# A three-layer graph network with a feed-forward block on one core: f32 tables and one f32 product per gathered tile, in place of three bf16 parts and two products

## Chip, core and metric

One core of one Trainium2 chip runs the whole program in one launch. The metric is the device time in microseconds. The kernel before has a median of 7058.9 us over three runs (7055.39 to 7071.32).

## The reference

12500 nodes with 256 features, 200000 edges sorted by destination. Three graph layers and one feed-forward block, both residual:

```python
def _sage_layer(x, src, dst, inv_deg, W_self, W_neigh, b):
    agg = jax.ops.segment_sum(x[src], dst, num_segments=N_NODES)
    mean = agg * inv_deg[:, None]
    return x @ W_self + mean @ W_neigh + b
h = relu(layer0(layernorm(x)));  h = relu(layer1(h));  h = layer2(h);  x = x + h
# then: x = x + gelu(layernorm(x) @ w1 + b1) @ w2 + b2, scaled, for the rows with the largest x @ wr
```

The destinations are drawn as 12500 u², so low-numbered nodes have far more edges than high-numbered ones.

## The kernel before

The nodes are worked on in 98 windows of 128 (NT). The edges are cut in 1563 tiles of 128, and the tiles in 391 blocks of four (GROUP). For each layer there is a table in DRAM with one row per node. GpSimd gathers, with one indirect DMA per tile (line 672), the 128 source rows of a tile into `gath`, a ring of 16 tiles (RING, four blocks). VectorE makes for each tile a one-hot matrix of 128 edges by 128 nodes of the window (lines 1223 and 1230), and TensorE adds the tile's rows to their nodes as the product of that one-hot with the gathered rows, into the PSUM bank `agg` of the window.

Products on f32 data are not used for this. Each f32 row x is held as three bf16 parts: high = bf16(x), middle = bf16(x - high), low = the rest, so a table row is 3 x 256 bf16, or 1536 bytes. A tile takes two products: line 890 multiplies the one-hot with high and middle (512 columns), line 892 with low (256 columns; 257 in layer 0, where the last column counts the edges of each node). In layer 0 the low product has a bank of its own, `lo`, which ScalarE copies out (line 1716) before the next window may clear it (lines 878 and 879).

Phase 0 loads x, layer-normalises it in batches of four windows into `resid` (ScalarE, line 1678), and makes the three parts: casts on ScalarE (lines 1684 and 1690), subtractions on VectorE (lines 1085 and 1094). Batches are stored to `table[0]` on ScalarE's DMA queue (line 1702), and the gathers begin when all are stored.

In the layers, each window w is worked on in a slot of a loop over windows: the products of window w's blocks, and beside them the finishing of windows w-1 to w-4. Layer 0 divides the sum by the degree in `mean_done` (lines 1243 to 1260). The layer's matrix products are TensorE's lines 731, 743, 756 and 718. A product's left half is the next layer's table row, its right half the part that the node adds to itself. `copy_product`, `copy_rest` and `store_parts` (ScalarE, lines 1588 to 1616: copy L1596, casts L1597 and L1604, a store of the f32 row to `rows_f32` and one of the three parts to the table) and `split_product` (VectorE, lines 1183 to 1197: subtractions L1191 and L1196, bias L1193) make the parts. In layers 1 and 2 `aggregate_done` adds high and middle sums to the rest in two steps (lines 1276 and 1284).

The blocks of a window run from `first` to `shared`, the block that the window border cuts. TensorE's and VectorE's loops (line 898 and below line 1230) take one block a turn, in two or four spans (`sub_spans`, line 416), between which other work of the slot is issued. The shared block stands behind the loops. Its gathered rows are used by both windows, its one-hots are made once for each. The one-hots of block b lie in ring place (b + w) % 4, an address worked out at run time by both engines. A block that is done raises `slots_free`. Before VectorE makes a block's one-hots it waits for `slots_free` to reach the block's number plus a base (2 in layer 0). GpSimd waits for the same semaphore before it gathers into a block's place, through a relay on SyncE's queue, which also loads the gather indices (lines 600 to 605).

Layer 0 makes in windows 2 to 33 a second thing: counts of edges between groups of nodes. VectorE makes one-hots for them (lines 1340 and 1342), TensorE multiplies (line 784), ScalarE copies out (line 1623). With them layers 1 and 2 do the first four windows as dense products (line 827) with the f32 rows read from `rows_f32`, and skip those windows' gathers: layer 0 has 1564 gathers, layers 1 and 2 have 1260 each. Layer 2 has the feed-forward block in its slots: line 959 (256 to 1024), gelu on ScalarE (line 1795), line 969 (1024 to 256). A last stage picks the rows and stores the result.

Of the kernel before, what the change touches and what calls it, by code (L numbers as in the profile page):

```python
# [7 lines left out]
ALU = mybir.AluOpType  # L8
# [6 lines left out]
P = 128  # L15
PARTS = 3
# [8 lines left out]
FIN_BUFS = 19  # L25
# [5 lines left out]
COUNT_AT = 2  # L31
COUNT_LOOPED = 6
# [4 lines left out]
def gnn_ffn_program(nc, x, src, dst, w_self, w_neigh, b_gnn, wr, br, w1, b1, w2, b2, out):  # L37
# [68 lines left out]
    table = [nc.dram_tensor(f"table{l}", (N, PARTS * D), BF16).ap() for l in range(LAYERS)]  # L106
    idx_dram = nc.dram_tensor("idx_dram", (P, PADDED + TURN_TILES), I32).ap()
    rows_f32 = [None] + [nc.dram_tensor(f"rows_f32_{l}", (N, D), F32).ap() for l in range(1, LAYERS)]
# [3 lines left out]
    with ExitStack() as ctx:  # L112
# [11 lines left out]
        gath = sb("gath", [P, RING, PARTS * D + 2], BF16)  # L124
        onehot = sb("onehot", [P, RING, P], BF16)
# [26 lines left out]
        lo_sb = [sb(f"lo_sb{p}", [P, D + 1]) for p in range(2)]  # L152
# [5 lines left out]
        def build_area(cols):  # L158
# [23 lines left out]
        split = [sb(f"split{p}", [P, PARTS, D], BF16) for p in range(2)]  # L182
# [21 lines left out]
               for area, bufs in ((dense[:], 6), (gath[:].rearrange("p r d -> p (r d)").bitcast(F32), 6), (dst_f[:], 1),  # L204
# [4 lines left out]
        FIN_AFTER_SUMS, FIN_AFTER_FFN = 6, 13  # L209
# [13 lines left out]
        agg_lo = lo0[:]  # L223
# [13 lines left out]
        flag = split[1][:].rearrange("p t d -> p (t d)").bitcast(F32)[:, 0:NT]  # L237
        rest4 = [hidT[p][:].rearrange("p k n -> p (k n)").rearrange("p (b d) -> p b d", d=D) for p in range(2)]
# [55 lines left out]
        y32_stored = [sem(f"y32_stored{p}") for p in range(2)]  # L294
# [17 lines left out]
        hi4_ready = sem("hi4_ready")  # L312
        rest4_ready = sem("rest4_ready")
        mid4_ready = sem("mid4_ready")
        lo4_ready = sem("lo4_ready")
        shift4_ready = sem("shift4_ready")
        half_added = sem("half_added")
        lo_added = sem("lo_added")
        lo_copied = sem("lo_copied")
        mid_added = sem("mid_added")  # L320
# [20 lines left out]
        hi_ready = sem("hi_ready")  # L341
        rest_ready = sem("rest_ready")
        self_ready = sem("self_ready")
        mid_ready = sem("mid_ready")
        lo_ready = sem("lo_ready")
# [290 lines left out]
        def _(pool):  # L636
# [17 lines left out]
            for layer in range(LAYERS):  # L654
# [4 lines left out]
                else:  # L659
                    for k in range(4):  # L660
                        pool.wait_ge(slots_stored[k], 16 * (1 + BATCHES // 4 + (k < 2)))
# [1193 lines left out]
```

## Time and profile before

| | |
|---|---|
| median of three runs | 7058.9 us |
| profiled execution | 7076.15 us |
| its span | 7074.4 us, so 1.8 us lie outside |
| mean granted TensorE clock | 0.802 |
| busy: TensorE, VectorE, ScalarE, GpSimd | 4579, 2607, 1085, 3887 us |

The page gives busy times per engine and per line. PE is the matmul part of TensorE, PEld its weight loads, DVE is VectorE, ACT ScalarE, POOL GpSimd, SP SyncE; a name with q behind it is the engine's sequencer. "<-" names what ended an idle time; "issue" means that the engine waited for nothing that the profile shows, "remote" that the release came from outside it. The stages in time: phase 0 to 149 us, layer 0 to 2940, layer 1 to 4870, layer 2 with the feed-forward block to 6970, the last stage to 7074.

### The profile page before, as it was taken

Reading aid. Unit: us, or ns where it says so; the run is one execution under the profiler, and the core shown is the slowest. Engines: PE = TensorE matmul, PEld = TensorE weight load, DVE = VectorE, ACT = ScalarE, POOL = GpSimd, SP = SyncE. Lnnn points to the kernel's source line nnn. Section 1 sums busy time; section 2 is a strip of 40 time slices with the busy share of each in tenths; the row PEclk is TensorE's granted clock in tenths of the full one; section 3 lists DMA queues with packets and bytes.
Section 4 is the critical chain, followed back from the end, with each engine's and each line's share of the span. In section 5 each row is a group of like instructions: output and inputs, shape, how many; then the busy total and the mean of one; then the engine's idle time right before and its main releaser. Section 6 shows DMA issues by size and latency. Waiting matters only on the chain.

```text
span 7074.4 us, 108443 instructions
## 1 busy us (share of the span) xinstructions
PE 4579.0 (65%) x20873; PEld 2778.3 (39%) x20874; DVE 2607.1 (37%) x6727; ACT 1084.7 (15%) x2649; POOL 3887.2 (55%) x4094
## 2 busy tenths in 40 slices
PE   1444555555667777646778656665578998788884
PEld 0112222222333344323456222222256776566664
DVE  6123333444423333311222332333333444455556
ACT  5000001111111112100000000000011223223331
POOL 1654544444466666566666666665666664555551
PEclk9666677777777888767888777777689998989997
DMA  7443444444455555446666555554456664444445
GB/s 232 133 116 109 123 121 124 126 126 126 129 143 146 150 151 151 145 135 185 192 197 208 157 151 147 155 156 137 133 181 187 194 197 116 135 139 136 125 129 181
DMA packets 564997, 1065.13 MB, mean 151 GB/s; under 512 B 154587, under 2 KB 361983, under 8 KB 558527
## 3 DMA queue, kind: packets, MB, share of 16 engines
q0 software_dynamic: 261376, 803.21, 39.9%
q10 hardware_dynamic: 196564, 228.51, 9.5%
q1 hardware_dynamic: 106987, 32.54, 2.0%
q8 instruction: 37, 0.61, 0.0%
q14 instruction: 33, 0.27, 0.0%
HBM read 928.09 MB, written 135.83 MB: 150 GB/s over the span
## 4 chain that ended last, share of the span: by engine, by line
issue 35%; PE 29%; DVEq 10%; DVE 7%; another core or an unknown queue 6%; POOL 5%; ACT 4%; DMA 1%; ACTq 1%; SPq 0%; POOLq 0%
PE agg L890 10%; POOL gath L672 5%; PE y L969 3%; PE agg L892 3%; PE lo L892 2%; PE hid L959 2%; PE y L731 2%; DVEq L1347 2%; PE lo L827 2%; DVEq L1240 1%; DVEq L1340 1%; ACT hidT L1795 1%; DVEq L1223 1%; PE hid L756 1%
## 5 line engine op out<-in xcount | busy, mean ns | idle before, releaser
L672 POOL DMA_INDIRECT gath<-table,idx_ring x4084 | 3885.7, 951 | 3052.3 <-issue 1344.3
L890 PE MATMUL agg<-gath,onehot 128*128 x5216 | 2262.5, 459 | 1392.3 <-issue 1036.4
L890 PEld LDWEIGHTS agg<-gath,onehot 128*128 x5216 | 578.4, 111 | 2287.9 <-issue 1999.8
L892 PE MATMUL agg<-gath,onehot 128*128 x3264 | 1000.4, 306 | 146.3 <-issue 141.5
L1230 DVE TENSOR_SCALAR onehot<-iota_row,window_base,dst_f 128x128 f32 x1632 | 481.2, 361 | 1020.6 <-issue 436.4
L892 PE MATMUL lo<-gath,onehot 128*128 x1952 | 664.2, 340 | 87.8 <-issue 83.0
L1223 DVE TENSOR_TENSOR onehot<-count_ps,dst_f 128x512 f32 x408 | 282.0, 691 | 1147.9 <-remote 607.4
L1223 DVE TENSOR_TENSOR onehot<-hid,dst_f 128x512 f32 x488 | 336.8, 691 | 837.2 <-issue 310.6
L969 PE MATMUL y<-w_sb,hidT 128*128 128x256 f32 x1568 | 420.6, 428 | 143.5 <-ACT hidT L1795 121.2
L892 PEld LDWEIGHTS agg<-gath,onehot 128*128 x3264 | 347.6, 107 | 335.4 <-issue 248.4
L959 PE MATMUL hid<-featT,w_gnn 128*128 128x128 f32 x3136 | 411.2, 290 | 53.9 <-issue 53.6
L959 PEld LDWEIGHTS hid<-featT,w_gnn 128*128 128x128 f32 x3136 | 393.0, 205 | 77.1 <-issue 67.7
L969 PEld LDWEIGHTS y<-w_sb,hidT 128*128 128x128 f32 x1568 | 330.9, 217 | 215.0 <-ACT hidT L1795 89.4
L784 PE MATMUL count_ps<-dense 128*128 x445 | 185.6, 431 | 352.2 <-issue 237.1
L1340 DVE TENSOR_SCALAR dense<-iota_row,dense 128x128 f32 x445 | 133.5, 300 | 577.5 <-issue 447.5
L892 PEld LDWEIGHTS lo<-gath,onehot 128*128 x1952 | 226.9, 116 | 234.3 <-issue 163.3
L827 PE MATMUL lo<-dense 128*128 128x256 f32 (+1 forms) x784 | 243.0, 433 | 22.7 <-issue 22.3
L1586 ACT ACTIVATE featT<-tp 128x256 f32<-128x256 f32 x196 | 73.4, 374 | 1132.7 <-remote 511.1
L1342 DVE TENSOR_SCALAR dense<-w_sb,dense 128x400 f32 x445 | 220.9, 496 | 56.1 <-issue 55.9
L1572 ACT ACTIVATE sd<-mv,eps 128x1 f32<-128x1 f32 x98 | 28.8, 294 | 1298.7 <-issue 790.9
L1795 ACT ACTIVATE hidT<-hid,b_sb 128x128 f32<-128x128 f32 (+1 forms) x784 | 212.5, 382 | 98.1 <-remote 73.8
L784 PEld LDWEIGHTS count_ps<-dense 128*128 x445 | 45.8, 104 | 462.1 <-issue 458.2
(193 smaller groups left out, 4169.3 us busy)
## 6 DMA issues: line engine op xcount, KB each, us to landing
gath<-table,idx_ring POOLq DMA_INDIRECT x4084
dense<-counts_dram ACTq DMA_DIRECT2D x50, 1024.0 KB
table<-split ACTq DMA_DIRECT2D x194, 192.0 KB
counts_dram<-dense ACTq DMA_DIRECT2D x16, 1600.0 KB
rows_f<-y ACTq DMA_DIRECT2D x194, 128.0 KB
dense<-rows_f ACTq DMA_DIRECT2D x48, 512.0 KB
table<-gath ACTq DMA_DIRECT2D x24, 768.0 KB, 3.5
xb<-x ACTq DMA_DIRECT2D x97, 128.0 KB
```

What stands on the lines that cost most here:

```text
L672: g.indirect_dma_start(gath[:, j, 0:PARTS * D], None, table[layer][:, :], bass.IndirectOffsetOnAxis(ap=idx_ring[:, h, i:i + 1], axis=0)).t ...
L784: return mm(count_ps[:, 0:GROUP_NODES * COUNT_COLS], low_hots[:, bass.ds(slot, 1), :], key_hots[:, bass.ds(slot, 1), :], stop=stop, **flags)
L827: last = mm(dense_ps[layer][w], counts[p][0:r, w * P:(w + 1) * P, c], node_rows[p][0:r, c, :], start=False, stop=ends, skip_group_check=True)
L890: mm(agg[p][:, 0:2 * D], oh, tile_rows[:, :, 0:2 * D], start=False, **flags)
L892: last = mm(low, oh, tile_rows[:, :, 2 * D:2 * D + lo_cols], start=False, **flags)
L959: last = mm(hid[:, j // 4, (j % 4) * P:(j % 4) * P + r], w1_sb[:, k, j * P:(j + 1) * P], featT[p][:, k, 0:r], start=(k == 0), stop=(k == K ...
L969: last = mm(y0[0:r, 0:D], hidT[p][:, j, 0:r], w2_sb[:, j, :], start=(j == 0), stop=(j == KH - 1))
L1223: v.tensor_tensor(onehot[:, bass.ds(pair, GROUP), :], ids.unsqueeze(1).to_broadcast([P, GROUP, P]), dst_f[:, bass.ds(tiles, GROUP)].unsque ...
L1230: last = v.tensor_scalar(onehot[:, bass.ds(pair, GROUP), :][:, j, :], iota_row[:], window_base[:, col(w)], dst_f[:, bass.ds(tiles, GROUP)] ...
L1340: v.tensor_scalar(low_hots[:, bass.ds(slot, 1), :], iota_row[:].unsqueeze(1), src_low[:, bass.ds(tile, 1)], None, ALU.is_equal)
L1342: v.tensor_scalar(key_hots[:, bass.ds(slot, 1), :], iota_keys.unsqueeze(1), group_base[:, col(g)], src_key[:, bass.ds(tile, 1)], ALU.add, ...
L1795: last = a.activation(hidT[p][:, j, 0:r], hid[:, j // 4, (j % 4) * P:(j % 4) * P + r], ACT.Gelu_apprx_tanh, bias=b1_sb[:, j:j + 1])
```

## The change

- `table` holds f32 rows of 1024 bytes. `rows_f32` is gone, and the dense step reads the table. `gath` and `onehot` are f32.
- A tile takes one f32 product of 256 columns (257 in layer 0) into `agg`. The bank `lo` for it, its clear, its copy and its wait are gone.
- Phase 0 stores from `resid`; the two casts and the two subtractions of each batch are gone. So are L1191, L1196, L1597, L1604, L1276, L1716, the second store and one half of the sum in `mean_done`.
- The one-hots lie in fixed places: two blocks for the loop, two for a single first block (one by the window's parity), two for the shared block. The loops take two blocks a turn (`pair_spans`); a block left over at the front is done alone behind an `If`.
- VectorE waits for `slots_free` in the loops alone, with a base of 3 in place of 2: in a loop it is at most two blocks ahead.
- The count groups of layer 0 lie in windows 4 to 35 (COUNT_AT 2 to 4, COUNT_LOOPED 6 to 4). The last stage has 18 buffers in place of 19.

```diff
-    table = [nc.dram_tensor(f"table{l}", (N, PARTS * D), BF16).ap() for l in range(LAYERS)]
+    table = [nc.dram_tensor(f"table{l}", (N, D), F32).ap() for l in range(LAYERS)]
-        gath = sb("gath", [P, RING, PARTS * D + 2], BF16)
-        onehot = sb("onehot", [P, RING, P], BF16)
+        gath = sb("gath", [P, RING, D + 2])
+        onehot = sb("onehot", [P, (2 + 2 + 2) * GROUP, P])
+        def pair_spans(eng, first, end, parts):
+            shift = parts.bit_length() - 1
+            cuts = [eng.snap((first * (parts - k) + end * k) >> shift) if k else first for k in range(parts)]
+            cuts = [eng.snap(cut + ((cut + end) & 1)) for cut in cuts]
+            return list(zip(cuts, cuts[1:] + [end]))
@@ TensorE, aggregate
-                if layer == 0:
-                    if not isinstance(n, int) or n:
-                        pe.wait_ge(lo_copied, n)
-                    mm(agg_lo[:, 0:1], zeros[:], ones_bf[:, 0:1], start=True, **free)
-                    pair = pe.snap(((b + w) % RING_BLOCKS) * GROUP)
                     pe.wait_ge(onehot_ready, b + w + pe_base[layer][0])
                     pe.wait_ge(rows_ready, b + pe_base[layer][1])
                     for j in range(GROUP):
-                        mm(agg[p][:, 0:2 * D], oh, tile_rows[:, :, 0:2 * D], start=False, **flags)
-                        low = agg[p][:, 0:D] if layer else agg_lo[:, 0:lo_cols]
-                        last = mm(low, oh, tile_rows[:, :, 2 * D:2 * D + lo_cols], start=False, **flags)
+                        last = mm(agg[p][:, 0:cols], onehot[:, slot * GROUP + j, :], tile_rows, start=False, **flags)
+                with pe.If(first < spans[0][0]):
+                    block_products(first, 2 + p).then_inc(slots_free, 1)
                     with pe.If(begin < end):
-                        with pe.Fori(begin, end) as b:
-                            block_products(b).then_inc(slots_free, 1)
-                block_products(shared, last_block=True).then_inc(agg_ready, 1)
+                        with pe.Fori(begin, end, 2) as b:
+                            for slot in range(2):
+                                block_products(b + slot, slot).then_inc(slots_free, 1)
+                block_products(shared, 4 + p, last_block=True).then_inc(agg_ready, 1)
@@ VectorE
-            dve_base = [2] + [dve.snap(dve_left * (RING_BLOCKS * layer) + (RING_BLOCKS * layer + 2))
+            dve_base = [3] + [dve.snap(dve_left * (RING_BLOCKS * layer) + (RING_BLOCKS * layer + 3))
-                    dve.wait_ge(slots_free, b + dve_base[layer])
+                    if looped:
+                        dve.wait_ge(slots_free, b + dve_base[layer])
```

## Rows read from the trace of the kernel before

**Rows 1.** The page: busy us (share) xinstructions, then the chain's shares by engine.
```profile
PE 4579.0 (65%) x20873; PEld 2778.3 (39%) x20874; DVE 2607.1 (37%) x6727; ACT 1084.7 (15%) x2649; POOL 3887.2 (55%) x4094
...
issue 35%; PE 29%; DVEq 10%; DVE 7%; another core or an unknown queue 6%; POOL 5%; ACT 4%; DMA 1%; ACTq 1%; SPq 0%; POOLq 0%
```

**Rows 2.** The page's groups: name xcount | busy, mean ns | idle before, releaser.
```profile
L672 POOL DMA_INDIRECT gath<-table,idx_ring x4084 | 3885.7, 951 | 3052.3 <-issue 1344.3
L890 PE MATMUL agg<-gath,onehot 128*128 x5216 | 2262.5, 459 | 1392.3 <-issue 1036.4
```

**Rows 3.** Stretches by stage: length, busy us of PE, PEld, DVE, ACT, POOL, clock, DMA.
```profile
385.00:1930.00 1545.00, 819.21 (x3181) 377.52 (x3180) 587.57 (x1402) 149.84 (x379) 738.74 (x774) 0.71 0.43 122
1930.00:2940.00 1010.00, 719.44 (x3527) 412.09 (x3525) 353.80 (x817) 184.31 (x533) 594.67 (x629) 0.83 0.50 145
2940.00:4870.00 1930.00, 1240.99 (x4733) 668.36 (x4733) 505.79 (x985) 130.17 (x392) 1192.41 (x1260) 0.78 0.57 167
4870.00:6970.00 2100.00, 1657.67 (x8934) 1250.93 (x8934) 926.69 (x2915) 510.48 (x1154) 1203.32 (x1260) 0.89 0.52 152
```

**Rows 4.** Timeline, POOL in layer 1: start, length, [idle before <- releaser].
```profile
4104.20 0.94 POOL L672 DMA_INDIRECT gath<-table,idx_ring  x1 [0.30 <-issue]
4105.45 0.94 POOL L672 DMA_INDIRECT gath<-table,idx_ring  x1 [0.30 <-issue]
4109.69 0.94 POOL L672 DMA_INDIRECT gath<-table,idx_ring  x1 [3.29 <-remote]
...
4139.83 0.94 POOL L672 DMA_INDIRECT gath<-table,idx_ring  x1 [3.26 <-remote]
```

**Rows 5.** Timeline, all engines, late layer 0, from 2014 us.
```profile
2014.44 0.10 PEld L892 LDWEIGHTS lo<-gath,onehot 128*128 x1 [1.29 <-issue]
...
2015.83 0.10 PEld L890 LDWEIGHTS agg<-gath,onehot 128*128 x1 [1.29 <-issue]
...
2017.22 0.10 PEld L892 LDWEIGHTS lo<-gath,onehot 128*128 x1 [1.29 <-issue]
```

**Rows 6.** Timeline, PE: pairs at the low clock, one at the high, f32 L969.
```profile
2021.28 0.64 PE L890 MATMUL agg<-gath,onehot 128*128 x1
...
2021.92 0.63 PE L890 MATMUL agg<-gath,onehot 128*128 x1
...
2023.52 0.38 PE L890 MATMUL agg<-gath,onehot 128*128 x1
...
2023.84 0.38 PE L890 MATMUL agg<-gath,onehot 128*128 x1
...
6331.98 3.71 PE L969 MATMUL y<-w_sb,hidT 128*128 128x256 f32 x16 [0.87 <-ACT hidT L1795]
```

**Rows 7.** Timeline, phase 0, DVE and ACT from 93 us.
```profile
93.73 1.22 DVE L1094 TENSOR_TENSOR gath<-hidT,gath 128x1024 bf16<-128x1024 f32 x1
...
96.08 1.05 ACT L1684 CAST gath<-resid 128x1024 bf16 x1
...
98.11 1.22 DVE L1094 TENSOR_TENSOR gath<-hidT,gath 128x1024 bf16<-128x1024 f32 x1
98.34 2.08 ACT L1678 ACTIVATE resid<-resid,shift,rstd  x4
```

**Rows 8.** PE and DVE groups of 385 to 1930 us, columns as in rows 2.
```profile
L890 PE MATMUL agg<-gath,onehot 128*128 x898 | 450.1, 517 | 266.6 <-issue 148.0 <-DVE onehot L1223 106.0 <-SPq L601 11.7
...
L1223 DVE TENSOR_TENSOR onehot<-hid,dst_f 128x512 f32 x224 | 154.6, 691 | 254.3 <-issue 163.4 <-remote 55.1 <-PE lo L892 23.4
L1340 DVE TENSOR_SCALAR dense<-iota_row,dense 128x128 f32 x445 | 133.5, 300 | 577.5 <-issue 447.5 <-PE count_ps L784 85.8 <-remote 40.0
L1259 DVE SCALAR_TENSOR_TENSOR feat<-agg,inv_deg,feat 128x256 f32<-128x256 f32 x33 | 16.0, 484 | 1.2
...
L1196 DVE TENSOR_TENSOR split<-rest,split 128x256 bf16<-128x256 f32 x30 | 12.7, 425 | 30.2 <-ACT split L1604 24.5 <-issue 5.7
L1191 DVE TENSOR_TENSOR rest<-y,split 128x256 f32<-128x256 f32 x30 | 12.4, 415 | 1.4 <-issue 1.4
```

**Rows 9.** L890 in late layer 0, layer 1 and layer 2, columns as in rows 2.
```profile
L890 PE MATMUL agg<-gath,onehot 128*128 x896 | 395.6, 464 | 192.2 <-issue 179.8 <-DVE onehot L1223 7.3 <-SPq L601 4.8
...
L890 PE MATMUL agg<-gath,onehot 128*128 x1632 | 715.9, 463 | 537.1 <-issue 465.0 <-DVE onehot L1223 35.8 <-SPq L601 28.0
...
L890 PE MATMUL agg<-gath,onehot 128*128 x1632 | 614.7, 411 | 172.9 <-issue 145.2 <-SPq L601 18.4 <-DVE onehot L1230 8.7
```

**Rows 10.** The page's DMA queues: kind: packets, MB, share of 16 engines.
```profile
q8 instruction: 37, 0.61, 0.0%
```

More of the change, by code:

```diff
@@ L181, in gnn_ffn_program @@
         featT = [sb(f"featT{p}", [P, KD, P]) for p in range(2)]
-        split = [sb(f"split{p}", [P, PARTS, D], BF16) for p in range(2)]
+        spare = sb("spare", [P, BATCH * D])
+        flag, cand = (sb(name, [P, NT])[:] for name in ("flag", "cand"))
         rest = sb("rest", [P, D])
@@ L871, in aggregate @@
                     pe.wait_ge(mean_ready, n - 1)
-                lo_cols = D + 1 if layer == 0 else D
+                cols = D + 1 if layer == 0 else D
                 free = dict(stop=False, skip_group_check=True)
@@ L1227, in block_onehots @@
                         return
-                    dve.sem_inc(dve_turn, 1)
                     for j in range(GROUP):
-                        last = v.tensor_scalar(onehot[:, bass.ds(pair, GROUP), :][:, j, :], iota_row[:],
+                        last = v.tensor_scalar(hots[:, j, :], iota_row[:],
                                                window_base[:, col(w)], dst_f[:, bass.ds(tiles, GROUP)][:, j:j + 1],
@@ L1233, in block_onehots @@
                     last.then_inc(onehot_ready, 1)
[L1234 to L1241 removed]
+                spans = pair_spans(dve, first, shared, len(between) + 1)
+                with dve.If(first < spans[0][0]):
+                    block_onehots(first, 2 + p)
+                for k, (begin, end) in enumerate(spans):
+                    if k:
+                        between[k - 1]()
+                    with dve.If(begin < end):
+                        with dve.Fori(begin, end, 2) as b:
+                            for slot in range(2):
+                                block_onehots(b + slot, slot, looped=True)
+                block_onehots(shared, 4 + p)
             def mean_done(n, p):
                 r = rows(n)
[L1246 to L1247 removed]
+                dve.wait_ge(agg_ready, n + 1)
+                v.tensor_scalar(deg[0:r, :], agg[p][0:r, D:D + 1], 1.0, None, ALU.max).then_inc(deg_ready, 1)
                 dve.wait_ge(deg_ready, n + 1)
@@ L1444, in _ @@
             low, exist = xb[1][:, 0:NT], rest[:, 0:NT]
[L1445 to L1446 removed]
+            flags = onehot[:].rearrange("p r d -> p (r d)")[:, 0:TRIALS * NT].rearrange(
                 "p (t n) -> p t n", n=NT)
[L1448 to L1449 removed]
             st = stats[0]
@@ L1785, in slot_layer1 @@
                 if exists(w - 3):
-                    split_store(2, w - 3, earlier(half, p, 3), 1 - p, part)
+                    copy_product(2, w - 3, earlier(half, p, 3), 1 - p)
+                    store_rows(2, w - 3, 1 - p, part)
             over_windows(act, 3, LOAD_LOOPS, slot_layer1)
@@ L1801, in _ @@
             for p in range(2):
[L1802 removed]
+                act.wait_ge(stored[p], 16 * NT)
             def slot_ffn(w, half, p, part):
```

207 lines of the change are left out of this document (42 added, 165 removed).

## Prediction

> **What bounds the kernel now.** I read the page first, then the stretches by stage, then the timeline at a few places. No engine is near full: TensorE's matmuls are busy 65% of the span and GpSimd 55%, and the chain that ended last is 35% "issue", 29% PE and 17% VectorE with its sequencer [rows 1]. So the costs to look at are those between operations, stage by stage. The one hard floor is the gathers. Back to back they start 1.25 us apart, 0.95 of it busy and 0.30 between [rows 4]; 4084 of them [rows 2] need 5105 us. Each stage stands above its own floor by a different amount: 385 to 1930 us holds 774 gathers, 968 us of 1545; late layer 0 has 629, 786 of 1010; layers 1 and 2 have 1260 each, 1575 of 1930 and of 2100 [rows 3]. The most that faster work around the gathers can give is therefore 577, 224, 355 and 525 us.
>
> What holds GpSimd back in layer 1 is seen in its timeline: runs of about a dozen gathers, and then a pause of 3.3 us until ring places come free [rows 4]. TensorE is late in freeing them, although its products are short. While the gathers go out in an unbroken row, its weight loads start 1.39 us apart, with 1.29 us of "issue" between loads of 0.10 us, and two loads and two products make one tile [rows 5]: 2.8 us per tile against 1.25 us per gather. Between such stretches the same pair takes 0.32 to 0.33 us at the high clock (2.4 GHz, granted 1.0) and 0.64 at the low one (1.2 GHz) [rows 6]. Over the run L890 has 1036.4 us of idle time that ended in "issue" [rows 2], by stage 148, 180, 465 and 145 us [rows 8, 9].
>
> From 385 to 1930 us the loop of count one-hots on VectorE is a second brake: 447.5 us of "issue" before L1340, and TensorE waits 106.0 us for one-hots [rows 8]. In layer 2 TensorE itself is the most loaded, 1657.67 of 2100 us [rows 3].
>
> **The change part by part.** The profiled execution took 7076.15 us, with a span of 7074.4 and 1.8 outside it; it is 17 us, or 0.24%, above the median. The sum below is made against 7076.15, and its difference is then taken from the median.
>
> Phase 0. A batch takes 98.11 - 93.73 = 4.38 us, a little more where VectorE waits [rows 7]. VectorE loses two subtractions of 1.22 and ScalarE two casts of 1.05 [rows 7]. What is left per batch is about 1.9 us of VectorE and 2.4 of ScalarE (2.08 of it L1678), and ScalarE is late next. That saves up to 2.0 us a batch. Some 21 of 25 batches stand after the loads of x, and the loads and stores (1 MB a batch in place of 1.3) also need their time, so I take 1.85: -39 us. Bounds: 0, if the loads of x set the pace, and -50 (25 x 2.0). The first gather waits for all stores, so this lands on the end in full.
>
> The product of a tile. Sixteen f32 records of 256 columns take 3.71 us, 0.232 each with their start-up, and a product is two records: about 0.43 us back to back at the high clock [rows 6], where the pair takes 0.325. At the low clock I double it to 0.86, against 0.64. So a tile costs +0.11 or +0.22 us. By the stage's clock, read as a mix of 1.0 and 0.5, the low level holds 58%, 34%, 44% and 22% of the four stages [rows 3]. With 898, 896, 1632 and 1632 tiles [rows 8, 9] the added TensorE time is 898 x 0.174 = 156, 896 x 0.147 = 132, 1632 x 0.158 = 258 and 1632 x 0.134 = 219 us, in all some 765 us.
>
> The issue of a tile. There is one product in place of two and one run-time address in place of two, and a loop turn serves two blocks. In a stretch like [rows 5] a tile then takes about 1.4 us where it took 2.8. About half of the "issue" idle before L890 goes: 74, 90, 232 and 73 us, 470 in all. Bounds: none of it, if the stretches merely go on longer, and all of it, if a tile at 1.4 us against a gather at 1.25 no longer falls behind by a ring of 16 tiles before the stretch ends.
>
> These two terms are of one size, +765 and -470, and which one counts depends on who waits. While GpSimd sets the pace, a longer product is hidden in TensorE's idle time: in layer 1, TensorE is busy 1241 of 1930 us, so 689 are free for 258 [rows 3]. The shorter issue acts exactly where GpSimd's pauses arise. By stage:
> - 385 to 1930: +156 and -74 on TensorE. VectorE loses L1191 and L1196 (0.42 each) and one sum step of 0.48 a window, 33 windows, -44 us, some 25 us of its waits for ScalarE's casts [rows 8], and loop turns; -85 in all. The two engines wait for each other in turn, so half of each side: +41 - 42, near 0. Bounds: +82 and -150.
> - late layer 0: +132 and -90, with most of the windows near the gathers' time: 0. Bounds: -95 and +60. The clear of `lo` and its wait for ScalarE's copy are in it, at nothing: the copy is off the path as long as TensorE is behind GpSimd.
> - layer 1: 355 us above its floor. Of the -232 I let 100 reach the end, since TensorE's other products in the slot stay as they are and have to be issued in the same stretches. Bounds: -280 and +60.
> - layer 2: the added 219 fall on an engine that is busy 79% of the stage and bounds the windows with feed-forward work; half of it, +110, less 60 of issue: +50. Bounds: -60 and +150.
> - the steps between layers: a shorter chain from the last product to the last stored row (two casts, two subtractions and their hops): -4 us each, -8. Bounds: 0 and -20.
> - the smaller edits at nothing: rows of 1024 bytes in place of 1536 (a gather's issue of 0.95 us, not its bytes, sets the pace), the dense step from the table, one buffer less at the end, the counts two windows later. If the buffer's cover is gone it costs one transfer, a few us. One-hots in f32: the f32 one-hot could take longer than 691 ns [rows 8] to write, up to twice that by its bytes, or no longer; VectorE is busy 506 of 1930 us in layer 1 [rows 3], which hides it.
>
> The new depth. VectorE may be two blocks ahead in a loop, where it could be three. TensorE needs 1.7 us (high) or 3.4 (low) for a block of f32 products (4 x 0.43 or 0.86), more than a VectorE operation and its issue; so it is covered outside the slow stretches. Queued behind the waiting one-hot are the slot's other VectorE steps, for which the matrix products wait.
>
> Sum: -39 + 0 + 0 - 100 + 50 - 8 = -97, so 6979 for a run like the profiled one; from the median, 7058.9 - 97 = 6962 us.
>
> **The rivals.**
> (a) Slow issue mostly goes. If a tile at 1.4 us keeps up with gathers at 1.25, GpSimd's pauses vanish in layer 1 and late layer 0 (-280, -120), the count stage gains 100 and layer 2 is even: with phase 0 about -540, near 6520; half of that, -290 or 6770, if it holds for layer 1 alone. For it: rows 4 and 5 fit each other, the pause following a dozen gathers. Against: waits, loop steps and the window's other products are issued as slowly as the products, and those do not halve. Chance 0.20.
> (b) The product counts in full. TensorE sets the pace where its clock is low and in layer 2, and the slow stretches stay as long, since they end with GpSimd's pause and not with TensorE's work. Then +82, +60, +60 and +150, less 47: +305, or 7364 at most; with two thirds of each, +190 or 7250. It decides from the point where less than a quarter of the "issue" idle goes. For it: layer 2's 79%, and a clock of 0.71 in the count stage [rows 3]. Chance 0.24.
> (c) The loss of one block of lead. In a slow stretch a block's one-hots and its products are issued at the same slow pace, and two fixed places make the engines take turns; 98 windows in each of three layers times half a micro-second, +150, would leave 7110. Rows 8 speak for it in the count stage (106.0 us), the 35.8 and 8.7 us in layers 1 and 2 [rows 9] against it. Chance 0.06.
> (d) More code in the loops. Two blocks a turn and a block behind an `If` lengthen each slot's program. In the trace the instruction queue moved 37 packets in the whole run [rows 10], so the loops over windows fetch next to nothing now. If each of some 147 turns of two windows had to fetch once, at between 1.29 us (one slow issue, [rows 5]) and 3.29 us (a pause of GpSimd, [rows 4]), that would be +190 to +480; with 2 us I take +300, or 7260. The Trainium skill (Runtime: NRT & Kernel Launch, Instruction fetch mechanics) says that a taken branch out of the resident pages stops the engine until its page is fetched; by that rule 37 packets mean that the loops stay resident, and the trace agrees. Chance 0.04.
> (e) Nothing moves: the terms cancel to within 0.2% (a measurement of this kernel tells about that much from no change). Chance 0.10.
>
> **How the numbers follow.** The forecast's own case, from -200 to -15 us, has 0.36. Faster by over 0.2%: 0.36 and 0.20 = 0.56; within: 0.10; slower: 0.24 + 0.06 + 0.04 = 0.34. For 8 in 10 the range leaves out the far half of (a) and the top of (b) and (d): 6640 to 7270. The forecast's own range is 6860 to 7045.
>
> **What would show it.** Right: the first gather near 110 us in place of 149; in layer 1 under 300 us of "issue" before the product, longer rows of gathers between pauses, and the stage some 100 us shorter; TensorE busier by 500 us or more; layer 2 longer by tens of us. A product near 0.43 us at the high clock and the one-hot still near 691 ns. Rival (a): stages 2 to 4 within 5% of their gathers' time. Rival (b): "issue" before the product as before, and every stage after phase 0 longer. Rival (c): VectorE's one-hot waiting for the product, and the product for the one-hot, by over 100 us more. Rival (d): hundreds of instruction packets. The forecast is wrong if the f32 product takes another time than L969's records, or if slow issue follows something else than how many instructions a tile needs.

## The result and the profile after

The changed kernel takes 7196.46 us (median of four runs, 7190.15 to 7201.56) against 7063.57 us for the kernel before, a ratio of 1.0188 (95% interval 1.017 to 1.0206). It is 1.9% slower, where 1.4% faster was forecast. The page of the profiled execution, its first lines and two groups:

```profile
span 7199.8 us, 96582 instructions
PE 5000.7 (69%) x20775; PEld 3888.9 (54%) x20776; DVE 2186.2 (30%) x5901; ACT 876.4 (12%) x2109; POOL 3886.9 (54%) x4094
...
q8 instruction: 43, 0.70, 0.0%
q14 instruction: 108, 0.88, 0.0%
...
L662 POOL DMA_INDIRECT gath<-table,idx_ring x4084 | 3885.4, 951 | 3167.4 <-PE agg L874 1323.6
L874 PE MATMUL agg<-gath,onehot 128*128 x10432 | 3045.9, 448 | 1247.2 <-issue 608.3
```

Against [rows 1, 2]: VectorE and ScalarE have 16% and 19% less to do, TensorE 9% more, and the gathers' busy time and number are the same. "Issue" before the product fell from 1036.4 to 608.3 us, but GpSimd's idle time rose from 3052.3 to 3167.4 us. The product of a tile is now two records, so 10432 of them.

The stretches by stage (same columns as [rows 3]; a stage begins with its first gather):

```profile
342.00:1969.00 1627.00, 909.31 (x3170) 609.54 (x3168) 540.09 (x1268) 117.47 (x282) 739.25 (x775) 0.72 0.28 81
1969.00:2962.00 993.00, 779.07 (x3449) 595.50 (x3449) 247.90 (x574) 121.09 (x334) 594.45 (x628) 0.89 0.33 94
2962.00:4844.00 1882.00, 1355.08 (x4733) 1014.45 (x4733) 373.13 (x700) 63.46 (x196) 1194.35 (x1261) 0.84 0.39 117
4844.00:7054.00 2210.00, 1766.08 (x8739) 1527.12 (x8739) 836.51 (x2757) 493.60 (x1110) 1202.10 (x1260) 0.89 0.35 104
```

The same gathers bound the same work in every kernel of this study, so each stage can be measured from the start of one gather to the start of another: gather 0 ends phase 0, and gathers 163, 937, 1564 and 2824 open the count stage, late layer 0, layer 1 and layer 2. Layer 2 is also cut in four segments of 315 gathers. Everything in this table, here and below, is in us:

| | phase 0 | first windows | counts | late layer 0 | layer 1 | layer 2 (its last two segments) | last stage |
|---|---|---|---|---|---|---|---|
| before | 149 | 236 | 1554 | 1001 | 1932 | 2067 (546, 547) | 135 |
| changed | 110 | 232 | 1627 | 993 | 1882 | 2210 (577, 639) | 146 |

So 39 us came from phase 0, as worked out, and 50 from layer 1, half of what was worked out; 73 were lost in the count stage, 143 in layer 2 and 11 in the last stage. What remains is to say what took the 216 of the count stage and layer 2.

### The profile page after: what moved, and what is told of

It reads as the page before. It is cut to its first block and busy times, and to the rows that moved or that the text cites. A ratio compares the mean times of both kernels' runs of the same rounds, so it can differ in the third digit from the quotient of the medians.

```text
span 7199.8 us, 96582 instructions
## 1 busy us (share of the span) xinstructions
PE 5000.7 (69%) x20775; PEld 3888.9 (54%) x20776; DVE 2186.2 (30%) x5901; ACT 876.4 (12%) x2109; POOL 3886.9 (54%) x4094
## 5 line engine op out<-in xcount | busy, mean ns | idle before, releaser
L662 POOL DMA_INDIRECT gath<-table,idx_ring x4084 | 3885.4, 951 | 3167.4 <-PE agg L874 1323.6
L874 PE MATMUL agg<-gath,onehot 128*128 x10432 | 3045.9, 448 | 1247.2 <-issue 608.3
L874 PEld LDWEIGHTS agg<-gath,onehot 128*128 128x128 f32 x10432 | 2276.6, 225 | 1881.1 <-issue 1493.0
L1183 DVE TENSOR_SCALAR onehot<-iota_row,window_base,dst_f 128x128 f32<-128x128 f32 x1632 | 453.5, 355 | 1087.7 <-PE agg L874 567.0
L1178 DVE TENSOR_TENSOR onehot<-hid,dst_f 128x512 f32<-128x512 f32 x488 | 321.0, 688 | 1085.5 <-remote 557.4
L1178 DVE TENSOR_TENSOR onehot<-count_ps,dst_f 128x512 f32<-128x512 f32 x408 | 269.7, 688 | 1250.0 <-remote 782.6
L945 PE MATMUL hid<-featT,w_gnn 128*128 128x128 f32 x3136 | 376.0, 277 | 19.9 <-issue 19.6
L945 PEld LDWEIGHTS hid<-featT,w_gnn 128*128 128x128 f32 x3136 | 370.8, 193 | 30.1 <-issue 24.4
L817 PEld LDWEIGHTS lo<-dense 128*128 128x128 f32 (+1 forms) x784 | 205.1, 327 | 39.2 <-issue 33.7
L746 PEld LDWEIGHTS hid<-hidT,w_gnn 128*128 128x128 f32 x1568 | 191.0, 192 | 56.0 <-issue 50.5
L746 PE MATMUL hid<-hidT,w_gnn 128*128 128x128 f32 x1568 | 193.0, 276 | 6.7 <-issue 5.3
L721 PE MATMUL y<-w_gnn,featT 128*128 128x512 f32 x392 | 191.3, 611 | 6.4 <-issue 4.9
L1539 ACT COPY dense<-count_ps 128x400 f32<-128x400 f32 x128 | 63.1, 493 | 963.8 <-PE count_ps L774 811.6
```

The lines of the kernel that those rows point to most:

```text
L662: g.indirect_dma_start(gath[:, j, 0:D], None, table[layer][:, :], bass.IndirectOffsetOnAxis(ap=idx_ring[:, h, i:i + 1], axis=0)).then_inc( ...
L721: last = mm(product_ps(phase, p)[0:r, :], featT[p][:, k, 0:r], w, start=(k == 0), stop=(k == KD - 1))
L746: last = mm(hT[:, m, 0:r], w_gnn[:, k % KD, 0, h * D + m * P:h * D + (m + 1) * P], zT[p][:, k, 0:r], start=(k == 0), stop=(k == 2 * KD - 1))
L817: last = mm(dense_ps[layer][w], counts[p][0:r, w * P:(w + 1) * P, c], node_rows[p][0:r, c, :], start=False, stop=ends, skip_group_check=True)
L874: last = mm(agg[p][:, 0:cols], onehot[:, slot * GROUP + j, :], tile_rows, start=False, **flags)
L945: last = mm(hid[:, j // 4, (j % 4) * P:(j % 4) * P + r], w1_sb[:, k, j * P:(j + 1) * P], featT[p][:, k, 0:r], start=(k == 0), stop=(k == K ...
```

## The experiments

The runs fell on several chips. The ratio is always to the median of the kernel before on the same chip. Two theories stood against each other: P, the f32 product's time on TensorE costs it; L, the loops' part costs it. The loops' part is the fixed places, the two blocks a turn and VectorE less far ahead; how far VectorE is ahead of TensorE is called its lead.

### The loops' part alone, the lead alone, a cheap product, early counts

`d`: the kernel before, with the fixed places, `pair_spans`, two blocks a turn and base 3; the parts and two products per tile stay. (For memory, `yw` shares the place of `split`; the run m below shares it too and loses nothing.)

```diff
-        onehot = sb("onehot", [P, RING, P], BF16)
+        onehot = sb("onehot", [P, (2 + 2 + 2) * GROUP, P], BF16)
@@ TensorE
-                        oh = onehot[:, bass.ds(pair, GROUP), :][:, j:j + 1, :]
+                        oh = onehot[:, slot * GROUP + j, :]
```

> The kernel before with the loops' part of the change alone: bf16 parts and two products per tile stay, but the one-hots lie in six fixed places, the loops take two blocks a turn and VectorE waits with base 3. Theory P (the f32 product's time on TensorE costs the 133 us): the loops' part does no harm, and fewer run-time addresses help a little, 6950 to 7060 us. Theory L (the loops' part costs it: two places in the loop make VectorE and TensorE take turns): 7100 to 7200 us, with VectorE's one-hot waits for the product raised by over 200 us as in the changed kernel.

Measured: 1.032 (1.0295 to 1.0345), 7397.31 us against 7177.21 on this chip, which is slower for every kernel. Alone, the loops' part costs more than the whole change.

`h`: the kernel before with `dve_base` 3 in place of 2.

```diff
-            dve_base = [2] + [dve.snap(dve_left * (RING_BLOCKS * layer) + (RING_BLOCKS * layer + 2))
+            dve_base = [3] + [dve.snap(dve_left * (RING_BLOCKS * layer) + (RING_BLOCKS * layer + 3))
```

> The kernel before, with one number changed: VectorE waits for slots_free with base 3 in place of 2, so it is one block less ahead; one block a turn and run-time places stay. Theory L (the lost lead): 7110 to 7200 us. Theory P (the product's time): within 20 us of before, 7045 to 7080 us.

Measured: 1.0253 (1.0229 to 1.0278), from one number. VectorE's waits in layer 2, first of the kernel before (its profile is from the first chip) and then of `h` (engine, line, what it waited for: us in total, times, longest):

```profile
DVE onehot L1230 <- issue: 436.4, 372, 10.1
DVE onehot L1230 <- remote: 351.1, 66, 13.9
DVE onehot L1230 <- PE agg L892: 232.2, 62, 15.5
```

```profile
DVE onehot L1230 <- PE agg L892: 596.5, 148, 13.7
DVE onehot L1230 <- issue: 293.1, 257, 10.2
DVE onehot L1230 <- remote: 289.8, 43, 13.8
```

The wait for TensorE's products rises by 364 us, from 62 waits to 148; the other two fall, so the three together rise by 160. Layer 2 takes 2235 us in `h` against 2067, and the count stage 1578 against 1554. The chip itself is part of that: `d` and `f` were run again on a chip with the first one's speed, and here they were 37 and 52 us longer in layer 2 and 16 and 15 in the count stage. What `h` lost lies mostly in layer 2.

`f`: the changed kernel with bf16 one-hots and a product that reads only the upper 16 bits of each f32 value. The lower halves are left out.

```diff
-        onehot = sb("onehot", [P, (2 + 2 + 2) * GROUP, P])
+        onehot = sb("onehot", [P, (2 + 2 + 2) * GROUP, P], BF16)
@@ TensorE
-                        tile_rows = gath[:, bass.ds(base, GROUP), :][:, j:j + 1, 0:cols]
+                        tile_rows = upper[:, bass.ds(base, GROUP), :, :][:, j, 0:cols, 1]
```

> The changed kernel with a cheap product: the one-hots are bf16 and each tile's product reads only the upper 16 bits of the f32 rows, as bf16 (a sum of truncated values: the lower halves are left out). Loops, places, gathers and bytes stay; a tile takes TensorE some 0.11 us at the high clock in place of 0.43. Theory P: the time falls by all of the 133 us and more, to 6750 to 6950 us, most of it in the count stage and layer 2. Theory L: it stays above 7100 us.

Measured: 0.9895 (0.9872 to 0.9918). So P is not wrong either: most of the product's time, taken away, is worth some 3% of the run (against the 1.0188 of the first chip). That is more than the time by which the change made the product longer; how much more, the second run of this kernel shows below.

`e`: COUNT_AT 2 and COUNT_LOOPED 6 in the changed kernel.

> The changed kernel with the count groups in windows 2 to 33 as before (COUNT_AT 2, COUNT_LOOPED 6) in place of 4 to 35. The windows' edges fall from the first window on, so the counts stand beside more gathers again. If their place is worth what the count stage lost (72 us longer than before), this gives back 30 to 72 us, 7125 to 7165 us; if place is indifferent and the stage's loss comes from product or loops, it stays within 20 us of 7196.

Measured: 7213.73 us, 1.0064 (1.0039 to 1.009); the microseconds that were expected don't apply to this chip, so the ratio counts. The changed kernel did not run on it; on two other chips of the same kind it had 1.0188 and 1.0197. The place of the counts is worth about 1% by that, but across chips.

### The same chip for all, and a chip of another kind

> The kernel before, unchanged, for its stages on the same chip as the runs beside it. Its stages should stand to each other as in its first profile; the second and third segments of layer 2 are what the lead theory speaks of.

> The changed kernel, unchanged, beside the others of this call. Ratio to before 1.012 to 1.022, as in the result (1.0188). It is the base for the two kernels behind it and for the early counts: if it stands above 1.0064 here too, the place of the counts is worth the difference.

> The changed kernel with more lead for VectorE: four loop places in place of two, chosen by the window's parity, and the first pair of a window made without the wait for slots_free, as the single first block and the shared block are already (one buffer less at the end pays for the memory). Loop waits behind it keep base 3. Theory L (lost lead): the late windows of layer 2 have hardly more than one pair, so their waits vanish; the time falls by 100 to 250 us, to 0.985 to 1.005 of before. Theory P (the f32 product's time): within 25 us of the changed kernel.

> The same as k_own_places, and the count groups in windows 2 to 33 as before. Theory L and the place of the counts act in different stages (layers 1 and 2, and windows 0 to 35 of layer 0), so the gains add: 0.973 to 0.995 of before. If they act on the same wait, it is no faster than the better of the two alone.

`k` and `ke` give VectorE lead back at the start of each window: its first pair of blocks is made without the wait. Behind it the loop keeps its base of 3 and two places a window, so within the loop the lead is still two blocks.

```diff
+        onehot = sb("onehot", [P, (4 + 2 + 2) * GROUP, P])
@@ VectorE
+                    if k == 0:
+                        with dve.If(begin < end):
+                            for slot in range(2):
+                                block_onehots(begin + slot, 2 * p + slot)
+                        begin = dve.snap(begin + 2)
```

Measured: before 5719.27 us, changed 1.0274 (1.0257 to 1.0291), k 1.0201 (1.0184 to 1.0218), ke 1.0131 (1.0114 to 1.0148). The same program took 1340 us less on this chip than on the first. The wait that the prediction rested on, TensorE's product for "issue", is nearly gone in the kernel before here. First the row of the first chip, then of this one:

```profile
PE agg L890 <- issue: 1036.4, 705, 9.2
```

```profile
PE agg L890 <- issue: 34.6, 93, 1.0
```

Counted over the trace of the first chip, register and branch instructions of 0.6 us or more on the sequencers of TensorE, VectorE and SyncE number some 2580, with a median of 0.70 us (the median of all of TensorE's register instructions is 0.06). With near neighbours joined they make some 400 slow stretches of 1955 us in all; the number of stretches depends on how near is near, the sum by some 5%. Below this is called slow issue. On this chip there is not one such instruction. The operations themselves take the same time on both (VectorE's one-hot L1223 691 ns, a gather 951 and 954 ns). The stages here:

| no slow issue | phase 0 | first windows | counts | late layer 0 | layer 1 | layer 2 (last two) | last stage |
|---|---|---|---|---|---|---|---|
| before | 149 | 206 | 1116 | 817 | 1623 | 1670 (430, 419) | 137 |
| changed | 110 | 204 | 1243 | 817 | 1596 | 1775 (445, 484) | 137 |
| k | 110 | 204 | 1204 | 815 | 1590 | 1774 (445, 484) | 139 |
| ke | 110 | 207 | 1162 | 809 | 1592 | 1775 (445, 484) | 139 |

Layer 1 is near its gathers' 1575 us for both. More lead at the start of a window and early counts each give about 40 us in the count stage, and neither moves layer 2 by 2 us. So layer 2 does not lack lead there. The 39 us that the lead gives in the count stage are given on a chip without slow issue. And the change costs more here than on the first chip, 127 us in the count stage and 105 in layer 2, so the change does not need slow issue to lose.

> The changed kernel, unchanged, as the base for the others of this call. On a chip whose register and branch instructions are never slow (no stretches of 0.70 us each while gathers run) the ratio to before should be near 1.027, on one that has them near 1.019.

> The loops' part alone (bf16, two products, fixed places, two blocks a turn, base 3), again. Where slow stretches exist it was 1.032 of before. Theory: its harm comes from VectorE's lost lead under slow issue, so on a chip without slow stretches it is within 1% of before (0.99 to 1.01), and on one with them again 1.025 to 1.04.

> The changed kernel with a bf16 product of the upper half of each f32 value (the lower halves are left out), again. Without slow stretches the f32 product's time is what costs, so the ratio falls from 1.027 to 0.96 to 0.985; with them the gain over the changed kernel is 2 to 3% as before (0.99 against 1.019).

> The kernel before with more lead: eight places for one-hots in place of four, and VectorE waits with base 1 in layer 0 and -2 in layers 1 and 2 in place of 2 (four blocks further ahead there). Taking one block of lead away cost 2.5% where slow stretches exist; if lead is what they eat, more of it gives 1 to 4% back there (0.96 to 0.99). Without slow stretches: 0.99 to 1.0. If lead is already enough, 1.00 on both.

These four fell on a chip with slow issue. Measured: changed 1.0197 (1.0166 to 1.0229), d2 1.033 (1.0307 to 1.0353), f2 0.9886 (0.9857 to 0.9915), m 0.9993 (0.9975 to 1.0012). Whether d, f and h behave otherwise without slow issue stays open. m, with eight places and a base smaller by 1 in layer 0 and by 4 in the others, shows that the kernel before had lead enough: less costs (h), more gives nothing.

| slow issue | phase 0 | first windows | counts | late layer 0 | layer 1 | layer 2 (last two) | last stage |
|---|---|---|---|---|---|---|---|
| changed | 110 | 230 | 1636 | 994 | 1882 | 2200 (566, 646) | 145 |
| d2, loops' part alone | 150 | 233 | 1588 | 998 | 1912 | 2261 (578, 702) | 147 |
| f2, cheap product | 110 | 226 | 1565 | 980 | 1874 | 2081 (519, 604) | 143 |

Changed minus f2 is 71 us in the counts, 14 in late layer 0, 8 in layer 1 and 119 in layer 2. It is not the price of the step from two bf16 products to one f32 product, but of more: at the high clock eight tiles of f2 take 1.08 us, against 3.70 in the changed kernel (the row is shown further on).

```profile
6745.81 1.08 PE L876 MATMUL agg<-gath,onehot 128*128 x8
```

The difference is 0.33 us a tile; the step from the pair (0.325 us) to the f32 product (0.43 to 0.46) is 0.11 to 0.14. The loops' part (d2 against the first chip's profile of before; the two chips have medians of 7074.47 and 7063.57) is +34 in the counts, -20 in layer 1 and +194 in layer 2. Going on from d2 to the whole change saves 96 us of median: 40 in phase 0, 30 in layer 1 and 61 in layer 2, against 48 lost in the count stage, where the later place of the counts is in it. With the fixed places there, one f32 product in place of two bf16 ones is a gain in layer 2. VectorE's wait for the product in layer 2, 232.2 us in the kernel before, is 565.2 in d2 and 561.0 in the changed kernel on this chip, the sign that theory L had named.

### Lead or lumps in layer 2, and what makes slow issue

> The changed kernel with loop places by the window's parity and the first pair of a window made without the wait for slots_free. Without slow stretches it gained 40 us in the count stage and nothing in layer 2. With slow stretches, theory L: the late segments of layer 2 fall by 50 to 100 us and the whole to 1.000 to 1.010 of before (the changed kernel 1.020). If layer 2 stays within 20 us, the lead isn't what the fixed places cost there, and the lumps of two blocks are.

> The same with the counts in windows 2 to 33. Against k2 the count stage falls by 40 to 80 us: 0.990 to 1.003 of before where slow stretches exist, 1.013 where not.

Measured: k2 1.0115 (1.0091 to 1.0139), ke2 1.0093 (1.0061 to 1.0125). k2 has 1565 us in the count stage (changed 1636) and 2215 in layer 2 (2200). The lead at the start of a window is worth 0.8%, all of it in the count stage, and nothing in layer 2; the early place adds nothing to it that can be told (1586). The count stage of the kernel before takes 1554 us, of the changed kernel 1627 and 1636, and three edits bring it back by themselves: k2 to 1565, the cheap product of f2 to 1565, the early counts of e to 1551. Their gains overlap, so the 73 us can't be shared out among them.

> The kernel before with one wait added on GpSimd: after each 8 gathers it waits until the last four have landed, so no row of gathers is longer than 8 and each ends with some 2.5 us of rest (1.56 us per gather on average, 6370 us for all). Theory S (slow issue arises in unbroken rows of gathers and ends when the last has landed): the slow stretches shrink from about 1950 us to under 600, and the time stays within 3% of before or falls, although every gather got dearer. If they arise from something else, they remain and the time rises by 5% or more. Where there are no slow stretches at all: 6400 us or more against 5720.

```diff
+                            if q % 2 == 1:
+                                pool.wait_ge(landed[q], it * (16 * GROUP) + land_base[q < LAST_BLOCKS])
```

Measured: 1.0398 (1.0368 to 1.0428), slower as a whole. But the slow stretches fell from 1955 to 610 us, in layer 1 from 628 to 26, and the count stage from 1554 to 1415. So the stretches do follow the rows of gathers, near the bound of 600 us that theory S had set, but not row length alone: of the slow instructions w8 keeps 38 of 833 in layer 1 and 405 of 734 in the count stage, with no row over eight in either. The "within 3%" does not hold: where the gathers themselves set the pace (layer 1, 2153 against 1932 us) the rests cost more than they bring.

Then the trace of the changed kernel was read again for layer 2. TensorE, late in it:

```profile
6938.67 3.70 PE L874 MATMUL agg<-gath,onehot 128*128 x16
6942.23 1.74 PE L945 MATMUL hid<-featT,w_gnn 128*128 128x128 f32 x12
...
6947.33 1.03 PE L874 MATMUL agg<-gath,onehot 128*128 x4
```

Sixteen records are eight tiles: both blocks of the window's pair stand ahead of the feed-forward products L945, where before there was one block on each side of them. (The row behind them is cut by the window of this view; it goes on to eight records, the shared block.) And GpSimd, just before:

```profile
6908.64 0.94 POOL L662 DMA_INDIRECT gath<-table,idx_ring  x1 [13.07 <-PE agg L874]
...
6917.40 0.95 POOL L662 DMA_INDIRECT gath<-table,idx_ring  x1 [0.30 <-issue]
6927.08 0.94 POOL L662 DMA_INDIRECT gath<-table,idx_ring  x1 [8.73 <-PE agg L874]
```

The kernel before, in the same layer:

```profile
6617.64 0.94 POOL L672 DMA_INDIRECT gath<-table,idx_ring  x1 [2.54 <-PE agg L892]
...
6624.21 0.94 POOL L672 DMA_INDIRECT gath<-table,idx_ring  x1 [1.88 <-remote]
...
6631.48 0.97 POOL L672 DMA_INDIRECT gath<-table,idx_ring  x1 [2.58 <-PE agg L892]
```

Before, GpSimd got four places at a time here and paused some 2 to 2.6 us; now it gets eight and pauses 8.7 to 13. Over the last segment, rows of exactly four gathers fall from 40 to 7, rows of eight rise from 15 to 33, and the pauses from 171 to 256 us in all. `p` puts the feed-forward products between the two blocks again, on TensorE alone:

```diff
+                if layer == 2 and parts == 2:
+                    mid = pe.snap((spans[0][0] * 3 + shared) >> 2)
+                    mid = pe.snap(mid + ((mid + shared) & 1))
+                    pair_loop(spans[0][0], mid)
+                    with pe.If(mid < shared):
+                        block_products(mid, 0).then_inc(slots_free, 1)
+                    between[0]()
+                    with pe.If(mid < shared):
+                        block_products(mid + 1, 1).then_inc(slots_free, 1)
+                    pair_loop(pe.snap(mid + 2), shared)
```

> The changed kernel with another order on TensorE in the windows of layer 2 without dense step: one pair of blocks straddles the feed-forward products of the slot (one block ahead of them, one behind), as single blocks did before; with one pair in the window both blocks stood ahead of them. VectorE's order and all places stay. Theory L2 (lumps: eight ring places come free at once, GpSimd pauses longer and runs longer): the last segments of layer 2 (566 and 646 us) fall by 40 to 90 us together, 1.007 to 1.014 of before. If the f32 product's time alone is what layer 2 lost, it stays within 15 us: 1.018 to 1.021.

Measured: 1.0146 (1.012 to 1.0173). The last segment fell from 646 to 556 us, near the 547 of before, and the rows of four are back (54). The third rose from 566 to 617. By the code `mid` leaves more blocks behind the feed-forward products than ahead of them in windows with several pairs, which may be why; no run shows it. Layer 2 as a whole: 2165 against 2200, and 2067 before. So the order of the pair makes the loss of the last segment, and undoing it this way is worth 35 us of layer 2; expected were 40 to 90 us for the two segments together, measured 39. It overlaps with the product's time, since f2 takes 42 us off the same segment with the order as it is.

> The kernel before, and in layer 0's gather turns 10 to 57 (the count stage) GpSimd waits after each 8 gathers until the last four have landed; elsewhere nothing is changed. w8, which waits everywhere, had a count stage of 1415 us against 1554. If that gain stands by itself: 0.978 to 0.988 of before where slow stretches exist, and 1.00 to 1.02 where they don't. If it was bought by the slower first windows, within 0.5% of before.

> The changed kernel with three edits: counts in windows 2 to 33, the straddling pair in layer 2, and the drained gathers in the count stage. By the stages: 7199 - 75 (place of the counts) - 50 (pair) - 100 (drained) = 6975, 0.985 to 0.99 of before, and not clearly below x. If the drained gathers and the place of the counts act on the same waits, 1.00.

`x` is the wait of w8 in the count stage alone, in the kernel before. `q` is the changed kernel with early counts, the straddling pair and the same wait.

```diff
+                    for a, b in ((0, 10), (10, 58), (58, FULL_TURNS)):
+                        with pool.Fori(a, b) as it:
+                            gather_turn(it, RING_BLOCKS, drained=a == 10)
```

Measured: x 6929.14 us, 0.9829 (0.9803 to 0.9856); q 6903.82 us, 0.9781 (0.9752 to 0.9811). By their ratios both beat both kernels. q was expected at 6975 us and came out 71 below; it is 25 us below x, and their ranges (6885.5 to 6904.8, 6918.37 to 6937.2) don't touch. What the wait alone is worth in the changed kernel was not run. The count stage of x, same columns as [rows 3]:

```profile
382.00:1800.00 1418.00, 842.52 (x3237) 396.16 (x3238) 594.02 (x1408) 152.97 (x385) 739.27 (x774) 0.73 0.47 133
```

The same gathers and the same work on every engine in 1418 us in place of 1554, by making GpSimd wait; the slow instructions of the stage fall from 734 to 394. Its rows of gathers, from the trace of x: eight, then a rest until the last has landed:

```profile
1000.98 0.94 POOL L672 DMA_INDIRECT gath<-table,idx_ring  x1 [3.44 <-issue]
...
1009.75 0.95 POOL L672 DMA_INDIRECT gath<-table,idx_ring  x1 [0.30 <-issue]
1013.62 0.95 POOL L672 DMA_INDIRECT gath<-table,idx_ring  x1 [2.92 <-DMA gath<-table,idx_ring]
```

Both ran on a chip with slow issue. On one without it the stage runs at 1116 us for 774 gathers, 1.44 us each, less than the 1.58 that the wait allows by the rows above (12.64 us for eight); there it would likely cost, which wasn't tried.

## Why the prediction was wrong

**Phase 0, -39.** Right: the first gather starts at 110.22 us in place of 149.26.

**The loops' part as a whole, entered as a gain only.** The sum has half of the "issue" for it as a gain, its depth at nothing, and its order not at all. By itself it costs 3.3%, 230 us of median (d2), 194 of them in layer 2; all the rest of the change gives 96 back. The depth and the order of the pair, below, are the two parts of it that runs take apart.

**The product of a tile, +765 in all.** Its price is right: sixteen f32 records, eight tiles, take 3.70 us at the high clock, 0.46 a tile with the start-up, where 0.43 was taken. What of the step from the pair to the f32 product reaches the end has no run of its own. Taken were 78 us in the count stage, 110 in layer 2 and nothing in layer 1; changed against f2 gives 71, 119 and 8, but f2 takes away more than twice as much time per tile. That the numbers agree is luck. From d2, where the pair is, to the whole change, layer 2 gets 61 us shorter, so there the longer product and the fewer instructions together are a gain and not the +50 of the sum. TensorE's busy time rose by 422 us and not by 500 or more, while its mean clock rose from 0.802 to 0.831.

**The issue of a tile, -470.** Half right. "Issue" before the product went from 148 to 77 us in the count stage and from 465 to 259 in layer 1, but from 145 only to 136 in layer 2:

```profile
L874 PE MATMUL agg<-gath,onehot 128*128 x1804 | 605.0, 504 | 201.1 <-DVE onehot L1178 116.7 <-issue 76.9 <-SPq L591 7.4
...
L874 PE MATMUL agg<-gath,onehot 128*128 x3264 | 962.1, 450 | 475.0 <-issue 258.9 <-DVE onehot L1178 190.9 <-SPq L591 23.8
...
L874 PE MATMUL agg<-gath,onehot 128*128 x3224 | 839.2, 410 | 199.8 <-issue 136.3 <-DVE onehot L1183 53.4 <-SPq L591 9.0
```

What went there came back in part as a new wait, for VectorE's one-hots: in layer 1 190.9 us where [rows 9] has 35.8, in layer 2 53.4 where it has 8.7. Layer 1 gained 50 us and not 100; that this wait took the other 50 is argued from these rows, not shown by a run of its own. On the chip without slow issue, where there was next to no such wait to save, layer 1 gained 27 us too, so the 50 may not all be this term's.

**The new depth, "covered outside the slow stretches".** This is the step that failed. It set TensorE's time for a block (1.7 or 3.4 us) against VectorE's operation, and took the lead of one block for free. Less lead costs 2.5% by itself in the kernel before (h). In the changed kernel lead given back at the start of each window is worth 71 us in the count stage with slow issue (k2, across chips) and 39 without a single slow stretch (k), so the depth was not covered outside them either. That the lead bridges slow stretches, in which both engines' instructions take about 0.70 us, is a likely reason for what h lost, but h was not run where there are none. h lost mostly in layer 2, k and k2 gained in the count stage alone: the one does not price the other, and what the lead within the loops costs the changed kernel stays open. The rival (c) had the mechanism, but priced it at 150 us and gave it 0.06, on the ground that TensorE hardly waited for VectorE before. Its sign came: the product's wait for the one-hot rose from 160 to 513 us over the run, and VectorE's for the product in layer 2 from 232.2 to 567.0. There was little wait before because the lead was there: a wait that a buffer hides is not in the profile until the buffer is gone.

**The order of the pair, costed at nothing.** `pair_spans` was read as a change of places and turns. It also moves a block from behind the feed-forward products to ahead of them, and frees places eight at a time. In the last segment that is 90 of the 91 to 98 us lost, and 35 us over layer 2 as p has it. Of the sum's +50 for layer 2, measured +143, this term was missing altogether. With p some 98 us of the 143 are left: no run takes the product's part of them from the loops'.

**The counts two windows later, at nothing.** Early counts gave 42 us in their stage on the chip without slow issue (k to ke), and nothing that can be told on one with it (k2 to ke2). By e it would be about 1% there, across chips. So it is a part of the loss of the count stage, for which 0 was taken and 73 measured, of a size that stays open.

**Rivals.** (a), slow issue goes and GpSimd is the bound: the slow stretches did shrink, to 1109 us, and the time did not follow. (Its "half of that, -290" is not half of 540, which is 270; nothing hangs on it.) (b), the product in full: the stages moved otherwise, since layer 1 fell. (d), code fetched each turn: the prediction read one of two instruction queues. They moved 43 and 108 packets in place of 37 and 33, not hundreds. The second stands at 36 in k2 and at 106 in ke2, which take 1882 and 1883 us in layer 1 and 2215 and 2208 in layer 2, so those 70 packets cost nothing that can be told.

**The rest.** Late layer 0, taken as 0, moved by -8. The steps between the layers (-8) no run separates. The last stage's +11 us has no cause shown; without slow issue it is 0. VectorE's one-hot takes 0.69 us in f32 as it did in bf16, as worked out.

## What to carry to other kernels

How far one engine is ahead of another is worth nothing in the profile until it is taken away: try the base of a wait by one in both directions before a change touches it. When a loop's turn grows, list for each window what now stands ahead of the work between the turns, and how many buffers come free at once. And a producer that runs ahead can be held back with profit where something else sets the pace: a wait for landings in one stage made the kernel before 1.7% faster (x).

## What the hardware showed that was not expected

- The same program takes 5719 us on one chip and 7047 to 7177 us on four others. The traces differ in the sequencers: some 2580 register and branch instructions of about 0.70 us on TensorE, VectorE and SyncE in the kernel before on the first chip, twelve on ScalarE, none on GpSimd, and none at all on the fast chip. The one-hots, the gathers and the time of the gathers' packets are the same on both.
- The stretches depend on the rows of gathers, but not on their length alone. With a rest after every eight (w8) they fall from 1955 to 610 us, and in layer 1 to 26. In the count stage half of the slow instructions stay, though no row is over eight there either; and the fast chip runs a row of 619 gathers in late layer 0 without one. Why a chip has them or not is open.
- With less work TensorE's clock is lower. With the bf16 product of f2 the mean granted clock is 0.724, with the f32 product 0.834 on the same chip, so part of what the cheap product saves in columns is likely lost again. The slow instructions rise as well, from some 1420 to 2200. The 223 us between the two are therefore not the product's time alone.
